# Fold, attention's end, norms and bank waits re-ordered in a fused two-layer kernel (RWKV-like mixing and latent attention with experts)

## What is computed

```
xn = LN(x);  s = two gated log-space scans(xn);  g = silu(expert FFN by nearest centroid(xn))
x  = x + s * g
xn = LN(x)
s  = mixing(xn)      # r, k, v, g, w by token shift and low-rank terms; state scan, 16 heads of 16x16
                     # y_t = r_t (S + u k_t v_t); S = w_t S + k_t v_t; o = silu(g) * LN16(y) @ oW.T
h  = xn + attention(rms(xn, w_ln1))   # 16 heads of 64, keys and values from 32 latent channels + 32 rotary
a  = h + shared expert(rms(h, w_ln2)) + top-2 of 8 experts(rms(h, w_ln2))
x  = x + s * silu(a)
```

## Time and profile before

| | |
|---|---|
| median of 3 runs | 2307.06 us (2302.12 to 2307.75) |
| the profiled execution | 2302.97 us, its span 2301.1 us |
| granted TensorE clock, mean | 0.957 |
| busy: TensorE, VectorE, ScalarE, GpSimd | 2074.5, 1808.8, 955.4, 822.6 us |

### The profile page before, as it was taken

One profiled execution on the slowest core, in us unless ns is written; L12 is line 12 of the kernel. 1 busy time (PEld: TensorE's weight loads), 2 busy tenths in 40 slices (PEclk: granted clock), 3 DMA queues, 4 the chain that ended last, 5 costly groups with the idle time before them and its releaser, 6 DMA issues. The chain is left out here.

```text
span 2301.1 us, 37278 instructions
## 1 busy us (share of the span) xinstructions
PE 2074.5 (90%) x11714; PEld 1242.7 (54%) x11715; DVE 1808.8 (79%) x2984; ACT 955.4 (42%) x2514; POOL 822.6 (36%) x666
## 2 busy tenths in 40 slices
PE   7997699995898999899899989998998999899887
PEld 4553599995445545544554455455445544554554
DVE  5997466663389979888987888798889878887986
ACT  3454244441256137424623561374247235612741
POOL 1335100001253254435433532544253335335430
PEclk9999799997799999999999999999999999999998
DMA  6453412114113012202211230122022212301210
GB/s 178 137 176 124 142 53 54 53 55 121 37 47 85 17 42 75 79 15 59 70 51 42 52 84 18 42 75 78 10 60 70 56 37 56 84 19 41 74 52 10
DMA packets 145727, 151.18 MB, mean 66 GB/s; under 512 B 47664, under 2 KB 105648, under 8 KB 145584
## 3 DMA queue, kind: packets, MB, share of 16 engines
q1 hardware_dynamic: 138288, 136.73, 21.6%
q0 software_dynamic: 3072, 8.41, 1.1%
q10 hardware_dynamic: 4224, 4.19, 0.6%
HBM read 121.71 MB, written 27.43 MB: 65 GB/s over the span
## 5 line engine op out<-in xcount | busy, mean ns | idle before, releaser
L2026 POOL TENSOR_TENSOR arena<-arena 128x512 f32<-128x512 f32 x256 | 340.7, 1332 | 587.0 <-DVE arena L1770 561.9
L1363 PE MATMUL bank<-arena 128*128 128x512 f32 (+2 forms) x1312 | 426.1, 479 | 15.8 <-ACT arena L1515 8.3
L1162 PE MATMUL bank<-arena 128*128 128x512 f32 (+2 forms) x768 | 355.7, 608 | 18.8 <-DVE arena L1687 10.3
L1770 DVE TENSOR_TENSOR_SCAN arena<-arena 128x512 f32<-128x512 f32 x256 | 368.5, 1440 | 2.6
L1363 PEld LDWEIGHTS bank<-arena 128*128 128x128 f32 x1312 | 239.7, 194 | 198.2 <-issue 152.2
L1556 ACT ACTIVATE arena<-bank,arena 128x128 f32<-128x128 f32 (+3 forms) x512 | 266.6, 531 | 170.2 <-DVE arena L1750 169.0
L1763 DVE TENSOR_TENSOR arena<-arena 128x512 f32<-128x512 f32 x256 | 228.8, 894 | 29.9 <-DMA arena<-values 29.8
L1222 PE MATMUL bank<-arena 64*128 64x128 f32 (+3 forms) x1024 | 208.1, 483 | 47.8 <-ACT arena L1556 44.7
L1162 PEld LDWEIGHTS bank<-arena 128*128 128x128 f32 (+2 forms) x768 | 137.4, 187 | 208.4 <-issue 170.3
L1565 ACT ACTIVATE arena<-bank 128x128 f32<-128x128 f32 (+3 forms) x512 | 197.8, 442 | 93.1 <-PE bank L1239 92.8
L1750 DVE TENSOR_REDUCE arena<-bank 128x2 f32<-128x256 f32 (+3 forms) x256 | 207.2, 809 | 36.9 <-PE bank L1225 36.1
(11 more groups left out here) (205 smaller groups left out, 2968.8 us busy)
## 6 DMA issues: line engine op xcount, KB each, us to landing
arena<-values SPq DMA_DIRECT2D x256, 256.0 KB, 3.4
arena<-in_L_attn_h SPq DMA_DIRECT2D x16, 512.0 KB, 4.9
arena<-in_W1T SPq DMA_DIRECT2D x8, 1024.0 KB, 5.0
arena<-in_W2T SPq DMA_DIRECT2D x8, 1024.0 KB, 9.0
sorted_rows<-arena SPq DMA_DIRECT2D x42, 128.5 KB, 10.0
arena<-sorted_rows SPq DMA_DIRECT2D x40, 128.5 KB, 2.1
arena<-in_b2row SPq DMA_DIRECT2D x40, 128.0 KB, 3.1
gate_rows<-arena SPq DMA_DIRECT2D x39, 128.0 KB, 1.7
```

Of the source, the lines that this page charges most:

```text
L1162: last = nc.tensor.matmul(dst[rows, :], w, x, start=(n == 0), stop=(n == len(pairs) - 1))
L1363: last = nc.tensor.matmul(dst[o], w, x, start=first, stop=last_one)
L1770: nc.vector.tensor_tensor_scan(state[n % STATES][:, 1:T + 1], proj["w"][:, m, :], kv[n % 2], VEC["init"][:, m * HD + j:m * HD + j + 1], AL ...
L2026: nc.gpsimd.tensor_tensor(prods[(n + 2) % PRODS], state[n % STATES][:, 0:T], proj["r"][:, m, :], ALU.mult).then_inc(prod_done, 1)
```

## The change

In words, by part:

- **Start.** SP loads kvb first, then s, x and qn; the expert weights wait until the gathers have landed. `fold` becomes `fold_values` (all of Wo, in two banks, by two groups, copied out by VectorE in two 128-row pieces) and `fold_queries` in two halves. TensorE runs the values' fold as soon as kvb is there, half of the queries' fold when qn is there, then turns the first sequence's rows, then the other half. ScalarE copies both turned halves out and scales the rms rows.
- **State.** `AHEAD` goes from 2 to 4 and `STEPPED` from 20 to 22: units 2 and 3 run before attention, 4 to 21 in its steps.
- **Attention's end.** One state reduction goes to the step behind the last scores, the mean and three of the four groups of the first Wo tile to the step after. Wo's four tiles have a bank each (the outputs `wo0` to `wo3`); the last group is added to tiles 0 and 1, then the variance, then to tiles 2 and 3. A reduction goes between the two halves of the turned rows in `experts`. VectorE centers first, and interleaves the two halves of its norm with units.
- **Norms.** ScalarE takes square roots straight from the bank, with eps as its bias. Scale and shift of the layer norm are joined to the multiplications around them. The scale of the head's rms rows goes from VectorE to ScalarE.
- **Next rows.** The next sequence's rows are turned behind the up products of expert 7 into banks of their own (`hx0`, `hx1`), and ScalarE copies both out. In the last sequence the turn is done too, on rows that are not used.
- **Banks.** `before` finds the last user of the very bank, across the seam of two sequences too, and the one wait for all of them goes.

The diff, cut to its core:

```diff
-STEPPED = 20
-AHEAD = 2
+STEPPED = 22
+AHEAD = 4
...
     def before(self, name):
-        n = self.at[name] - self.nbank
-        return self.names[n] if n >= 0 else None
+        old = [x for x in self.names[:self.at[name]] if self.bank(x) == self.bank(name)]
+        return old[-1] if old else None
...
+        if e == ME - 1:
+            yield from (("hx0", "a"), ("hx1", "a"))
...
-POST = ([("mean0", "v"), ("wo0", "v"), ("wo1", "v"), ("var0", "v"), ("xc0", "v"), ("xc1", "a"), ("gate", "v")]
+POST = ([("mean0", "v"), ("wo0", "v"), ("wo1", "v"), ("var0", "a"), ("wo2", "v"), ("wo3", "v"), ("xc0", "v"), ("xc1", "a"),
+         ("gate", "v")]
...
# SP
+            load(kvb_w, io["kvbT"].rearrange("p (g c) -> p g c", g=GROUPS))
+            sp.dma_start(s_in, ...)
             sp.dma_start(x_in, ...)
-            sp.dma_start(s_in, ...)
-            load(qn_w, ...)
-            load(kvb_w, ...)
+            sp.dma_start(qn_w, io["qnT"].rearrange("p (g c) -> p g c", g=GROUPS)).then_inc(qn_in, 16)
...
+            sp.wait_ge(g_loaded, 64)
             for e in range(ME + 1):
...
# TensorE
+                elif table is pre and b:
+                    old = [x for x in post.names if post.bank(x) == pre.bank(name)][-1]
+                    pe.wait_ge(post_read[post.reader[old]], post.read(b - 1, old))
...
+            def fold_values():
+                for half in range(2):
+                    for i in range(HGROUP):
+                        rows = slice(ND * i, ND * i + ND)
+                        for g in (2 * half, 2 * half + 1):
+                            last = nc.tensor.matmul(fold_bank[half][rows, (g % 2) * D:(g % 2 + 1) * D], kvb_w[rows, g, :], wo_w[rows, g, :],
+                                                    start=True, stop=True)
+                    last.then_inc(vo_mm, 1)
...
                 lora_a("vk", 0, 2)
-                pe.wait_ge(v_read2, len(post.order["v"]) * b + 1)
                 lora_a("rg", 2, 2)
...
                 for i in range(LAG, PSTEPS + LAG + 1):
                     if i < PSTEPS:
                         scores(b, i)
-                    if i == PSTEPS + LAG:
+                    if i == PSTEPS + 1:
                         pe.wait_ge(y_read, 2 * b + 1)
-                        pe.wait_ge(s_exp, STEPS * b + STEPS)
                         result(b, "mean0", [(full, mean_m, y[:, 0, :], True, True)], bank[post.bank("mean0")])
+                        pe.wait_ge(y_out, GROUPS * b + GROUPS - 1)
+                        wo(0, early)
+                        turn_probs(b, i - LAG)
+                    if i == PSTEPS:
+                        reduce_state(b, STEPPED // 4 - 1)
...
                 spread_inverse(b, GROUPS - 1)
+                for i in range(1, NT):
+                    wo(i, early)
                 pe.wait_ge(y_out, GROUPS * b + GROUPS)
-                for half in range(2):
-                    wo(half, 0, [GROUPS - 1])
-                    wo(half, 1, range(GROUPS))
+                wo(0, [GROUPS - 1])
+                wo(1, [GROUPS - 1]).then_inc(made2, 2)
                 pe.wait_ge(sq_done, 2 * b + 1)
                 result(b, "var0", [(full, mean_m, sq[0], True, True)], bank[post.bank("var0")])
-                reduce_state(b, STEPPED // 4)
+                wo(2, [GROUPS - 1])
+                wo(3, [GROUPS - 1]).then_inc(made2, 2)
...
                 for half in range(2):
+                    if half:
+                        reduce_state(b, STEPPED // 4)
                     pe.wait_ge(xc_done, 2 * b + half + 1)
...
-                    elif not final:
-                        pe.wait_ge(a_read2, post.read(b, last_g))
-                        pe.wait_ge(hid_done, post.read(b, last_u))
-                        turn_head(b + 1)
+                    if e == ME - 1:
+                        if not final:
+                            pe.wait_ge(xn_done, b + 2)
+                        for k in range(KD):
+                            begin(b, f"hx{k}", post, post_read)
+                            turn_head(k).then_inc(made2, 1)
...
-            turn_head(0)
             pe.wait_ge(weights_in, 16 * NW)
-            pe.wait_ge(xnT_left, 1)
-            pe.wait_ge(xnT_right, 1)
-            fold(0)
-            pe.wait_ge(vo_folded, HGROUP)
-            fold(1)
+            fold_values()
+            pe.wait_ge(qn_in, 16)
+            fold_queries(0)
+            pe.wait_ge(xn_done, 1)
+            for k in range(KD):
+                turn_head(k).then_inc(xn_turned, 1)
+            fold_queries(1)
...
# ScalarE
+            def scale_head(b):
+                act.wait_ge(rms_done, b + 1)
+                for i in range(NT):
+                    last = nc.scalar.activation(xb[:, i, :], xn[:, i, :], ACT.Copy, scale=rms[:, i:i + 1])
+                last.then_inc(xb_done, 1)
...
             def root_last(b):
-                act.wait_ge(last_read, 4 * b + 1 + 2)
-                nc.scalar.activation(inv[1], inv[1], ACT.Sqrt).then_inc(inv_done, 1)
+                act.wait_ge(last_mm, 4 * b + 2)
+                nc.scalar.activation(inv[1], whole[:, :], ACT.Sqrt, bias=eps_d[:, 0:1]).then_inc(last_read, 1)
...
-                nc.scalar.activation(inv[0], inv[0], ACT.Sqrt).then_inc(inv_done, 1)
+                take2(b, "var0", inv[0], ACT.Sqrt, bias=eps_d[:, 0:1]).then_inc(a_read2, 1)
...
+                    if e == ME - 1:
+                        for k in range(KD):
+                            act.wait_ge(made2, post.made(b, f"hx{k}"))
+                            turned_head(k).then_inc(a_read2, 1)
                 if not final:
-                    right_head(b + 1)
+                    scale_head(b + 1)
...
# VectorE
             def ln_scale(b, m):
-                nc.vector.tensor_tensor(y[:, m, :], y[:, m, :], inv[m], ALU.mult).then_inc(ln_step, 1)
...
+                nc.vector.scalar_tensor_tensor(y[:, m, :], y[:, m, :], VEC["ln_w"], inv[m], ALU.mult, ALU.mult).then_inc(ln_step, 1)
...
+                outer(b, 3)
                 if ended is not None:
                     gate_rows(ended, 1)
                     residual(ended)
+                scan(b, 2)
                 for name in QKV:
                     m = int(name[-1]) if name != "lat" else 0
+                    if name == "q2":
+                        unit(b, AHEAD - 1)
...
-                for n in range(STEPPED, EARLY - 1):
-                    unit(b, n)
+                center()
+                unit(b, STEPPED)
+                scale_values(b, GROUPS - 1)
                 scan(b, EARLY - 1)
-                scale_values(b, GROUPS - 1)
-                center()
-                outer(b, EARLY)
-                unit(b, EARLY)
...
+                add_rows(0)
+                outer(b, EARLY)
+                norm_rows(0)
+                add_rows(1)
+                scan(b, EARLY)
+                norm_rows(1)
...
-                    elif e == 4:
-                        ln_inv(b, 0)
                     elif e == 5:
                         read_out(b, 1)
+                        ln_inv(b, 0)
+                    elif e == 6:
                         ln_scale(b, 0)
-                    elif e == 6:
-                        ln_affine(b, 0)
                     elif e == 7:
                         center_last(b)
+                    elif e == 8:
                         ln_gate(b, 0)
-                    for at, part in ((1, head_gate), (2, head_sum), (3, head_stats), (5, head_norm), (6, head_rms), (7, head_lerp)):
+                    for at, part in ((1, head_gate), (2, head_sum), (3, head_stats), (4, head_norm), (6, head_ms), (7, head_lerp)):
...
# GpSimd
                     if n == 1:
                         g.wait_ge(a_read, pre.read(b, "pr_r1"))
-                        for k in range(AHEAD):
-                            product(b, k)
+                        product(b, 0)
+                        product(b, 1)
+                    elif n == 3:
+                        product(b, 2)
+                        product(b, 3)
```

190 lines of the change are left out of this document (87 added, 103 removed).

## The result

The changed kernel takes 2272.6 us (median of 4, 2269.6 to 2276.8) where the kernel before takes 2305.1: a ratio of 0.9861, 95% interval 0.9838 to 0.9883. It is faster by 1.4%, and the time lies inside the range of 2226 to 2277, near its upper end, but outside the 2238 to 2264 that the sum gave itself. The profiled execution is the slowest of the four, 2276.78 us.

The account below looks back on a forecast made before the run. TensorE was taken as the bound nearly everywhere, with its idle time and half-clock stretches to win. Terms -27.4 - 23 - 11.9 + 5.6 + 2.5 + 0.5 = -53.7 from 2302.97 gave 2249.3, put at 2250 us; range 2226 to 2277, the sum's own 2238 to 2264.

Parts of the forecast that it names:

- rival B: Attention's end gives nothing: serial norm chain, wait moves to VectorE's add, 23 us back, total 2273; chance 0.18.
- my own signs of being wrong: Stage before attention beyond 50.5 us, folds waiting for the gathers, or PEclk falling in the end as before.
- 1, the start: Before the last stage's first product: folds laid around the turn, gathered rows sooner; -27.4 us, bounds 24.4 and 31.
- 2, attention's end: Behind the last scores up to the gate: waits filled, clock kept up; -2.9 us x 8 = -23, bounds 0 and 4.3.
- 4, the moved units: Two state units moved into VectorE's waits ahead of the scores: +0.7 us x 8 = +5.6, bounds -0.5 and 3.
- rival C: Slower: both units delay the rotations at full price and the clock falls; 70 us instead of 5.6, total 2315; chance 0.04.
- 3, the seam: Between experts and next sequence: wait before the turn goes, first product's wait shrinks; -1.7 us x 7 = -11.9.
- 5, the clock: Behind the gate logits: one more clock fall than now; +2.5 us, bounds -10 and +10.
- 6 and the bank wait: Norms and tail: shorter norm passes in the experts give nothing, sum +0.5 us; removing the single bank wait gives nothing.

Follow-up runs that it names:

- no_gather_wait: The changed kernel without SP's wait for the gathers ahead of the 27 expert loads: 2269.7 us, ratio 0.9826.
- units_at_end: The changed kernel with no unit moved ahead of the scores (AHEAD = 2, STEPPED = 20), the reduction one step later: 2280.2 us, ratio 0.9887.
- fill_both: The changed kernel with useless TensorE products in the chain to the gate logits and before the variance of y's second half: 2256.1 us, ratio 0.9783.
- seam_early: The changed kernel with the seam's mean, centering and shifted differences begun sooner, same work: 2252.2 us, ratio 0.9748.
- fill_gate: The changed kernel with useless TensorE products in the idle time of the chain to the gate logits: 2259.3 us, ratio 0.9802.
- one_wait: The changed kernel with the single wait for all of VectorE's bank reads put back: 2272.4 us, ratio 0.9874.
- fold_after: The changed kernel with the first sequence's rows turned in front of all folds: 2274.9 us, ratio 0.9877.

## Why the prediction was right, and where it was wrong

The range held and the direction was right; the gain was forecast 1.65 times too large. That the range held is partly luck. The moved units and the clock together cost 25 us more than forecast, and the end gave 7 more than its term; with the forecast 23 the time would have been 2280, outside the range. The total is also the one of rival B, 2273, whose mechanism did not come: the end gave 30 us, and the units and the clock took it back. And one of my own signs of being wrong was met: the stage before attention grew beyond 50.5 us, to 51.1 to 51.4, in five of eight sequences (50.8 in two before). Step by step:

**1, the start,** right in size: 27.4 forecast, 24.3 measured, or 26.1 counted from the end of the stage before. The gathered rows came 14.0 us behind that stage, not 11.5; I had put down their lateness to the experts' weights, and no_gather_wait shows those to be worth 1 to 3 us; in the changed kernel the rows still came 2.5 us later than forecast. The query weights came late too. What made up for it was that the records of the first half of the fold ran in 6.21 us and not 7.2.

**2, attention's end,** right in sign and in mechanism, and too small: 30.0 over both stages against 23. The forecast 10.0 us became 8.5, with 0.25 us left of the waits and not 0.7, and no half clock. What I had missed is that this step hangs on step 4. The reduction can fill the first wait only if its units are done sooner, and I gave the moved units a price and no credit: units_at_end keeps the re-ordered products and wins 2.5 us of the 30.0. The norm chain idles 4.0 us and not 3.1, though the stage's length of 13.5 was close (13.88).

**4, the moved units,** the term that was most off: 5.6 forecast, 21.3 measured. I took 0.7 us a sequence, from an outer product at its mean of 0.89 us, and 1.8 if all were long. Measured are 2.2 at the scores, where neither kernel has a fall in them, and 0.58 before them, 2.8 in all, near my upper bound of 3. Each of the four passes was priced alone against the gap in front of it; what counts is that three of the four ran long and together they overfill the gaps, 6.9 us in 4.5, that GpSimd's rotations get longer too (1.27 to 2.2 us), and that both delays reach the same rotations. No run takes GpSimd's work away from there, so how much of it is the contention and how much the passes themselves is read from their durations alone. The rule of the Trainium skill (SBUF — State Buffer, "Who interferes with whom") was the better guide: three of the four passes ran long, the residual beside them took 1.59 us against 1.32, and rival C's place was right, with a third of its price. By the rule alone I had 1.8.

**3, the seam,** the mechanism right and the size wrong: 0.7 us a sequence between the shortest stages, not 1.7. The changed kernel's has a fall of 3.4 us in it, but fill_both shows the same 57.92 without one. I said that the wait for GpSimd's square may grow, and did not charge it; it took back 1.1 of what the turn's move gave. seam_early shows that this chain, not TensorE's work, held the stretch, and that another 2.4 us lay in it.

**5, the clock,** the other term that was far off: 2.5, or 3.6 with the last sequence's turn of 1.06, against 12.2. Time at half clock in the eight sequences is 84 us where it was 86. It left the end of attention, where TensorE idled much anyway, and went behind the gate and to the first products of a sequence, where TensorE is busy throughout and every half-speed product counts. I had the fall behind the gate as a small addition and not as the place to which the fall moves. fill_gate and fill_both show the cause: with TensorE kept at work in the chain 20 us of the 57 in the experts go, and with the seam filled too 43.

**6 and the bank wait:** one_wait shows nothing, as forecast. No run takes out the norms' shorter passes alone, so that they give nothing is not shown. Rival B was right about where the chain would be late, but the end paid in spite of it.

## What to carry to other kernels

When idle time of TensorE is closed in one place, ask where its clock will fall next: a stall in front of dense work costs its own length and can cost a half-speed stretch behind it. Useless products in a wait that can't be closed are worth a try, since they cost nothing while they fit. Useful work fills a wait only if its inputs are there in time, so look for the part of the change that makes them so before you give it a price alone. Before work is moved into the idle time of an engine, add up the whole stretch with the neighbour that it contends with, on both sides, and see who queues behind; and before a wait is filled, follow its releaser one step further back.

## What was not expected of the hardware

TensorE ran 2.8 us of useless products in each sequence's norm chain without the stage growing by more than 0.01 us, and the kernel got 0.6% faster. In fold_after the clock fell back to half at 569.3 with TensorE busy for 3.40 of the 3.40 us before and 4.28 of the 4.30 behind, in a run of 32x32 products without a gap; and in the kernel before such folds ran at half clock for 21.7 us, busy 21.59 of them. And beside a two-input pass of the other engine, one of VectorE and GpSimd ran long: VectorE's scan 1.28 to 2.29 us, GpSimd's rotation 1.27 to 2.29. At 1458.80 the scan that had started first kept its 1.27 us and the rotation took the 2.29.
